# Attention block on one core: another split of the first image's preparation over the engines

## The reference

```python
h = x.reshape(B, 32, 4, N); h = (h - mu) * rsqrt(var + 1e-6)      # group norm, 32 groups of 4 channels
h = h * gamma + beta
q, k, v = w_qkv @ h + b_qkv                                        # each 128 x 1024
attn = softmax(q^T k / sqrt(128))                                  # 1024 x 1024
out = x + w_proj @ (attn @ v) + b_proj
```

## Time and profile before

| what | us |
|---|---|
| median of 3 runs | 132.26 |
| lowest, highest | 130.9, 132.26 |
| the profiled execution's own time | 131.82 |
| its span | 129.8 |
| TensorE busy in the span | 114.6 (88%) |
| VectorE, ScalarE, GpSimd busy | 93.9, 87.9, 85.4 |

### The profile page before, as it was taken

The page is one execution under the profiler, slowest core; times in us unless marked ns, Lnnn a source line. Parts: engine busy times, 40 slices in busy tenths (PEclk is TensorE's granted clock), DMA queues, the critical chain, the costliest instruction groups (busy, mean ns, idle before and its releaser), DMA issues.

```text
span 129.8 us, 3100 instructions
## 1 busy us (share of the span) xinstructions
PE 114.6 (88%) x1161; PEld 80.6 (62%) x1161; DVE 93.9 (72%) x242; ACT 87.9 (68%) x121; POOL 85.4 (66%) x60
## 2 busy tenths in 40 slices
PE   0599887988998999999989999999899999987671
PEld 0373544556775677667646776776467767767550
DVE  3659799999856967998569579776695797774222
ACT  1304429999778787877986878879868788785000
POOL 6010004879999897999759888998657666788200
PEclk9999999999999999999999999999999999999999
DMA  3692000797999999999999999999999999999990
GB/s 94 170 346 119 0 3 17 146 123 147 192 153 187 184 197 129 240 191 192 149 224 194 187 192 200 179 146 234 190 169 132 243 192 114 197 232 155 179 246 20
DMA packets 70670, 21.43 MB, mean 165 GB/s; under 512 B 68352, under 2 KB 69120, under 8 KB 70656
## 3 DMA queue, kind: packets, MB, share of 16 engines
q1 hardware_dynamic: 69888, 20.98, 89.9%
q10 hardware_dynamic: 704, 0.26, 0.8%
q0 software_dynamic: 64, 0.00, 0.0%
HBM read 2.36 MB, written 2.10 MB: 34 GB/s over the span
## 4 chain that ended last, share of the span: by engine, by line
PE 49%; DVE 23%; DMA 9%; ACT 7%; SPq 6%; issue 2%; ACTq 0%
DVE row_max L432 10%; PE scores L617 7%; DMA ptT<-p_hl 6%; PE o_ps L637 6%; PE scores L619 6%; PE scores L618 6%; PE o_ps L633 5%; PE o_ps L632 5%; SPq L232 4%; DVE t_lo L421 4%; DMA wqkv_sb<-in_L_conv_w_qkv_dram 3%; PE o_ps L643 3%; ACT probs L343 3%; DVE out_sb L453 3%; ACT p_hl L350 2%
## 5 line engine op out<-in xcount | busy, mean ns | idle before, releaser
L285 POOL TENSOR_TENSOR p_hl<-probs,p_hl 128x1024 f16<-128x1024 f32 x32 | 68.1, 2130 | 27.0 <-ACT p_hl L350 26.7
L432 DVE TENSOR_REDUCE row_max<-scores 128x1 f32<-128x1024 f32 x32 | 39.1, 1222 | 19.3 <-PE scores L619 19.1
L343 ACT ACTIVATE probs<-scores,exp_bias,esc 128x1024 f32<-128x1024 f32 x32 | 38.5, 1202 | 19.2 <-DVE exp_bias L435 19.2
L350 ACT ACTIVATE p_hl<-probs 128x1024 f16<-128x1024 f32 x32 | 33.8, 1057 | 1.0
L632 PE MATMUL o_ps<-v_hi,ptT 128*128 128x128 f16 x256 | 32.0, 219 | 0.4 <-DVE v_lo L427 0.4
L633 PE MATMUL o_ps<-v_lo,ptT 128*128 128x128 f16 x256 | 32.0, 219 | 0.0
L617 PE MATMUL scores<-z_hi,t_hi 128*128 128x512 f16 x64 | 24.3, 379 | 2.8 <-DVE t_lo L421 1.7
L632 PEld LDWEIGHTS o_ps<-v_hi,ptT 128*128 128x128 f16 x256 | 25.0, 98 | 2.3 <-issue 0.8
L633 PEld LDWEIGHTS o_ps<-v_lo,ptT 128*128 128x128 f16 x256 | 25.0, 98 | 0.2
L619 PE MATMUL scores<-z_hi,t_lo 128*128 128x512 f16 x64 | 24.3, 379 | 0.0
L618 PE MATMUL scores<-z_lo,t_hi 128*128 128x512 f16 x64 | 24.3, 379 | 0.0
(11 more groups left out here) (109 smaller groups left out, 134.0 us busy)
## 6 DMA issues: line engine op xcount, KB each, us to landing
out_dram<-out_sb SPq DMA_DIRECT2D x7, 256.0 KB, 2.6
x_sb<-in_x_dram SPq DMA_DIRECT2D x3, 512.0 KB, 4.8
ptT<-p_hl SPq DMA_TRANSPOSE x64, 3.4
x_sb<-in_x_dram SPq DMA_DIRECT2D x2, 256.0 KB, 3.3
out_dram<-out_sb SPq DMA_DIRECT2D x1, 192.0 KB, 2.0
wqkv_sb<-in_L_conv_w_qkv_dram ACTq DMA_DIRECT2D x1, 128.0 KB, 4.0
wqkv_sb<-in_L_conv_w_qkv_dram ACTq DMA_DIRECT2D x1, 64.0 KB, 3.5
wp_sb<-in_L_conv_w_proj_dram ACTq DMA_DIRECT2D x1, 64.0 KB, 3.8
```

The lines of the kernel that those rows point to most:

```text
L285: nc.gpsimd.tensor_tensor(p_hl[:, g % RING, 1], probs[:, g % RING], p_hl[:, g % RING, 0], ALU.subtract).then_inc(plo_ready, 1)
L343: nc.scalar.activation(probs[:, g % RING], scores[:, g % SLOTS], ACT.Exp, bias=exp_bias[:, g:g + 1], scale=esc[:], accum_out=row_sum[:, g: ...
L350: nc.scalar.activation(p_hl[:, g % RING, 0], probs[:, g % RING], ACT.Copy).then_inc(phi_ready, 1)
L432: nc.vector.tensor_reduce(row_max[:, g:g + 1], scores[:, g % SLOTS], AX_X, ALU.max).then_inc(max_ready, 1)
```

## The change

It rearranges the preparation of image 0 and parts of tiles 0 to 4.

- Queues: x's first half, gamma, beta, b_q, Wp and Wv are issued on SP; Wq with Wk and x's second half on ScalarE's queue.
- TensorE has six filler matmuls ahead of everything (FIRST_WARM = 6), and WARM_UP is 8. group_mean(0) moves ahead of the c products, group_var(0) ahead of Wp's transposition.
- z of image 0: ScalarE makes both high halves straight from x, with nmr = -mean * rstd as bias and rstd as scale. VectorE computes z and z_lo of the first half, GpSimd those of the second half, and nmr.
- A's high half, ct, w_mat, esc and neg_esc go from VectorE to ScalarE. g_diag, w_diag and W's halves (by way of w_n, float32) go from VectorE to GpSimd.
- t of image 0's first 128 columns is a part of its own, in `misc[:, 1, 0:P]`; the other 384 of the first half follow, and the second half comes behind score tile 0. Semaphore counts of t shift by one (t_part), those of z by z_part.
- The maximum of W, w_inv and bo move into tiles 0 and 1 of the loop.
- The v products of both halves of image 0 are together in tile 2. The statistics of image 1: channel_stats(1, 1) in tile 2 instead of 1, group_mean(1) in tile 3 instead of 2, group_var(1) in tile 4 instead of 3. One of the two KEEP_WARM groups goes.

The core of the diff (declarations, the removed counterparts on VectorE and changed counts are left out):

```diff
 def _(sp):
-    for half in range(2):
-        cols = slice(half * HALF, (half + 1) * HALF)
-        sp.dma_start(x_sb[:, cols], x_d[0, :, cols]).then_inc(x_first[half], 16)
+    w_d = w_qkv.rearrange("(t o) c -> o t c", t=3)
+    sp.dma_start(x_sb[:, 0:HALF], x_d[0, :, 0:HALF]).then_inc(x_first[0], 16)
+    sp.dma_start(gamma_c[:], col(gamma)).then_inc(gcol_loaded, 16)
...
+    sp.dma_start(wp_sb[:], w_proj).then_inc(wp_loaded, 16)
+    sp.dma_start(wqkv_sb[:, 2], w_d[:, 2]).then_inc(wv_loaded, 16)
...
-    sp.wait_ge(gcol_loaded, 16)
+    sp.wait_ge(x_first[1], 16)
...
+    pool.wait_ge(gcol_loaded, 16)
+    pool.wait_ge(consts, 1)
+    nc.gpsimd.tensor_scalar(g_diag[:], ident32[:], gamma_c[:], None, ALU.mult).then_inc(gdiag_ready, 1)
...
+    pool.wait_ge(rstd_ready, 1)
+    pool.wait_ge(mean_ready, 1)
+    nc.gpsimd.tensor_tensor(nmr[:], neg_mean[:, 0:1], rstd[:, 0:1], ALU.mult).then_inc(nmr_ready, 1)
...
+    nc.gpsimd.tensor_scalar(z32[:, HALF:N], x_sb[:, HALF:N], neg_mean[:, 0:1], rstd[:, 0:1],
+                            ALU.add, ALU.mult).then_inc(z_second, 1)
+    pool.wait_ge(z_second, 1)
+    pool.wait_ge(zhi_ready, 2)
+    nc.gpsimd.tensor_tensor(z_lo[:, HALF:N], z32[:, HALF:N], z_hi[:, HALF:N], ALU.subtract
+                            ).then_inc(zlo_second, 1)
...
+    pool.wait_ge(wmax_ready, 1)
+    nc.gpsimd.tensor_scalar(w_diag[:], ident32[:], w_max[:, 0:1], None, ALU.mult).then_inc(wdiag_ready, 1)
+    pool.wait_ge(winv_ready, 1)
+    pool.wait_ge(wmat_ready, 1)
+    nc.gpsimd.tensor_scalar(w_n[:], w_mat[:], w_inv[:], None, ALU.mult).then_inc(wn_ready, 1)
+    pool.wait_ge(wn_ready, 1)
+    nc.gpsimd.tensor_copy(w_hi[:], w_n[:]).then_inc(whi_ready, 1)
+    pool.wait_ge(whi_ready, 1)
+    nc.gpsimd.tensor_tensor(w_lo[:], w_n[:], w_hi[:], ALU.subtract).then_inc(w_ready, 1)
...
-    act.dma_start(gamma_c[:], col(gamma)).then_inc(gcol_loaded, 16)
...
-    act.dma_start(wqkv_sb[:, 2], w_d[:, 2]).then_inc(wvp_loaded, 16)
-    act.dma_start(wp_sb[:], w_proj).then_inc(wvp_loaded, 16)
+    act.dma_start(x_sb[:, HALF:N], x_d[0, :, HALF:N]).then_inc(x_first[1], 16)
...
+    act.wait_ge(nmr_ready, 1)
+    for half in range(2):
+        cols = slice(half * HALF, (half + 1) * HALF)
+        nc.scalar.activation(z_hi[:, cols], x_sb[:, cols], ACT.Identity, bias=nmr[:], scale=rstd[:, 0:1]
+                             ).then_inc(zhi_ready, 1)
+    act.wait_ge(ainv_ready, 1)
+    act.wait_ge(amat_ready, 1)
+    nc.scalar.activation(a_hi[:], a_mat[:], ACT.Copy, scale=a_inv[:]).then_inc(ahi_ready, 1)
+    act.wait_ge(craw_ready, 1)
+    nc.scalar.activation(ct[:], c_raw[:], ACT.Copy, scale=a_inv[:]).then_inc(ct_ready, 1)
...
+    nc.scalar.activation(w_mat[:], scores[:, 1, HALF:HALF + P], ACT.Copy, scale=gamma_c[:]
+                         ).then_inc(wmat_ready, 1)
...
+    act.wait_ge(t_psum, 1)
+    act.wait_ge(ct_ready, 1)
+    nc.scalar.activation(t_hi[:, 0:P], misc[:, 1, 0:P], ACT.Identity, bias=ct[:]).then_inc(thi_ready, 1)
...
+    act.wait_ge(amax_safe, 1)
+    nc.scalar.activation(esc[:], a_max[:, 2:3], ACT.Copy, scale=1.0 / math.sqrt(P)).then_inc(esc_ready, 1)
+    nc.scalar.activation(neg_esc[:], a_max[:, 2:3], ACT.Copy, scale=-1.0 / math.sqrt(P)
+                         ).then_inc(esc_ready, 1)
...
+    dve.wait_ge(z_ready, 1)
+    dve.wait_ge(zhi_ready, 1)
+    nc.vector.tensor_tensor(z_lo[:, 0:HALF], z32[:, 0:HALF], z_hi[:, 0:HALF], ALU.subtract
+                            ).then_inc(zlo_ready, 1)
...
+    dve.wait_ge(thi_ready, 1)
+    nc.vector.scalar_tensor_tensor(out=t_lo[:, 0:P], in0=misc[:, 1, 0:P], scalar=ct[:], in1=t_hi[:, 0:P],
+                                   op0=ALU.add, op1=ALU.subtract).then_inc(tlo_ready, 1)
...
         if g == 0:
+            dve.wait_ge(wmax_psum, 1)
+            nc.vector.tensor_reduce(w_max[:, 1:2], o_ps[:, 1, P:2 * P], AX_X, ALU.max).then_inc(wmax_all, 1)
+            dve.wait_ge(wmax_all, 1)
+            nc.vector.tensor_scalar(w_max[:, 2:3], w_max[:, 1:2], 1.0 / V_MAX, TINY, ALU.mult, ALU.max
+                                    ).then_inc(wmax_safe, 1)
+            dve.wait_ge(wmax_safe, 1)
+            nc.vector.reciprocal(w_inv[:], w_max[:, 2:3]).then_inc(winv_ready, 1)
+        if g == 1:
             t_low(0, 1)
-        if g == 1:
+            dve.wait_ge(bo_psum, 1)
+            dve.wait_ge(o_loaded, 32)
+            nc.vector.tensor_tensor(bo[:], bp_c[:], o_ps[:, 0, 0:1], ALU.add).then_inc(bo_ready, 1)
             channel_stats(1, 0)
+        if g == 2:
             channel_stats(1, 1)
-        if g == 2:
+        if g == 3:
             group_mean(1)
-        if g == 3:
+        if g == 4:
             group_var(1)
         if s in (2, 3) and b < B:
             v_low(b, s - 2)
                          ).then_inc(var_psum, 1)
...
+    pe.wait_ge(const_warm, 1)
+    pe.wait_ge(const_dve, 3)
+    for _ in range(FIRST_WARM):
+        nc.tensor.matmul(scores[:, 1, 0:HALF], ones16[:], warm[:], start=True, stop=True)
...
+    pe.wait_ge(const_dve, 5)
+    group_mean(0)
...
-    group_mean(0)
+    group_var(0)
...
+    pe.wait_ge(zlo_ready, 1)
+    pe.wait_ge(a_ready, 1)
+    nc.tensor.matmul(misc[:, 1, 0:P], a_hi[:], z_hi[:, 0:P], start=True, stop=False)
+    nc.tensor.matmul(misc[:, 1, 0:P], a_hi[:], z_lo[:, 0:P], start=False, stop=False)
+    nc.tensor.matmul(misc[:, 1, 0:P], a_lo[:], z_hi[:, 0:P], start=False, stop=True).then_inc(t_psum, 1)
...
+        if g == 0:
+            t_products(0, 1)
+            pe.wait_ge(wdiag_ready, 1)
+            pe.wait_ge(amax_all, 1)
+            nc.tensor.matmul(o_ps[:, 1, P:2 * P], ones32[:], w_diag[:], start=True, stop=True
+                             ).then_inc(wmax_psum, 1)
+        if g == 1:
+            pe.wait_ge(wraw_ready, 1)
+            pe.wait_ge(o_loaded, 32)
+            nc.tensor.matmul(o_ps[:, 0, 0:1], w_raw[:], beta_c[:], start=True, stop=False)
+            nc.tensor.matmul(o_ps[:, 0, 0:1], wpT[:], bv_c[:], start=False, stop=True).then_inc(bo_psum, 1)
+        if g == LAG:
+            group_var(1)
         if g > LAG:
...
-            if s in (1, 2):
-                if g < TILES:
-                    pe.wait_ge(w_ready, 2)
-                pe.wait_ge(tlo_ready, b * 2 + s)
+            if g == 2:
+                pe.wait_ge(w_ready, 1)
+                for half in range(2):
+                    pe.wait_ge(tlo_ready, t_part(0, half))
+                    v_products(0, half)
+            if s in (1, 2) and b >= 1:
+                pe.wait_ge(tlo_ready, t_part(b, s - 1))
...
-            if g in (2, 3):
-                if g == 2:
-                    group_mean(1)
-                else:
-                    group_var(1)
+            if g == 3:
+                pe.wait_ge(bo_ready, 1)
+                group_mean(1)
...
```

More of the change, by code:

```diff
@@ L30 @@
 V_MAX = 4.0
-WARM_UP = 6
+FIRST_WARM = 6
+WARM_UP = 8
 KEEP_WARM = 4
@@ L79, in attention_block @@
         c_abs = sb("c_abs", [P, 1])
+        nmr = sb("nmr", [P, 1])
+        w_n = sb("w_n", [P, P])
         ct = sb("ct", [P, 1])
@@ L143, in attention_block @@
         araw_ready = sem("araw_ready")
+        esc_ready = sem("esc_ready")
+        bo_ready = sem("bo_ready")
+        ct_ready = sem("ct_ready")
         amat_ready = sem("amat_ready")
@@ L202, in stat, with z_part, t_part @@
             return o_ps[:, 0, 2 * P + which:2 * P + which + 1] if b < 2 else misc[:, which, 0:1]
+        def z_part(b, half):
+            return b * 2 + half if b else 1
+        def t_part(b, half):
+            return b * 2 + half + 2
         def wait(eng, s, value):
@@ L326, in t_high @@
             def t_high(b, half):
[L327 to L331, removed]
+                act.wait_ge(t_psum, t_part(b, half))
+                first = P if b == 0 and half == 0 else 0
+                nc.scalar.activation(t_hi[:, b * N + half * HALF + first:b * N + (half + 1) * HALF],
+                                     misc[:, half, first:HALF], ACT.Identity, bias=ct[:]).then_inc(thi_ready, 1)
             def v_high(b, half):
@@ L418, in t_low @@
             def t_low(b, half):
[L419 to L422, removed]
+                dve.wait_ge(thi_ready, t_part(b, half))
+                first = P if b == 0 and half == 0 else 0
+                cols = slice(b * N + half * HALF + first, b * N + (half + 1) * HALF)
+                nc.vector.scalar_tensor_tensor(out=t_lo[:, cols], in0=misc[:, half, first:HALF], scalar=ct[:],
+                                               in1=t_hi[:, cols], op0=ALU.add, op1=ALU.subtract
+                                               ).then_inc(tlo_ready, 1)
             def v_low(b, half):
@@ L590, in t_products @@
             def t_products(b, half):
-                pe.wait_ge(zlo_ready, b * 2 + half + 1)
-                cols = slice(b * N + half * HALF, b * N + (half + 1) * HALF)
-                nc.tensor.matmul(misc[:, half], a_hi[:], z_hi[:, cols], start=True, stop=False)
```

(12 more changed lines are left out.)

92 lines of the change are left out of this document (26 added, 66 removed).

## The result

| | before | after |
|---|---|---|
| median of the runs, us | 131.53 (20 runs, 130.54 to 132.93) | 132.94 (20 runs, 131.79 to 133.80) |
| profiled execution, us | 131.82 | 133.07 |
| its span, us | 129.8 | 131.3 |
| first row maximum | 17.18 | 15.90 |
| last row maximum | 114.89 | 116.34 |

The ratio is 1.0105, with an interval of 1.008 to 1.013: about one percent slower. The forecast was 133.2. The last three rows of the table are the handiest reading: the start gains 1.28 us, the loop loses 2.73. From the last row maximum to the span's end it is 14.9 and 15.0, so nothing happens there.

A forecast was written before the change was run, and what follows sets the result against it. Bound by one dependent path to 17.18, VectorE and ScalarE to 27.5, then nearly gapless TensorE until 108.08. The start gains 1.4, but the late variance delays values(2) by 1.4: 131.82 + 1.4 = 133.2, range 132.4 to 134.4 (55%).

The forecast's parts named there:

- The start's gain: Image 0's preparation, up to the first row maximum: forecast at 15.8 instead of 17.18, 1.4 us earlier.
- gamma's new way: At the start, gamma queued behind x's first half, its diagonal on GpSimd: booked at 0, with 0.3 either way.
- z's new route for nothing, under the block: Image 0's z saves about a microsecond but lies under the filler block, which covers 2; booked at nothing.
- The two outcomes of the shared port: Image 0's z on VectorE and GpSimd: mutual delay between zero and one z operation, 0.54, staying under the block.
- var_eps at D0 + 12.6: Image 1's variance on VectorE starts 12.6 us behind the first row maximum (D0), at 28.4 instead of 26.37.
- the sum of 3.45: Work newly standing on VectorE between the first row maximum and image 1's var_eps, added to the 9.19 us before.
- The three queues: TensorE, GpSimd, ScalarE wait for image 1's var_eps: values(0) plus 1.0, values(2) plus 1.4 (taken), exp(4) hidden.
- One microsecond late stays so: Loop behind values(2): TensorE is full, so 1.4 us late stays 1.4 us late until SP's tail.
- The rule "end = 131.82 + D0 - 14.4": Whole kernel: end follows the first row maximum D0; the change pays only if D0 falls below 14.4.
- Rival (a): Start: early fillers raise the clock for good, first row maximum 13.0 to 13.9, time 130.9; chance 27%.
- Rival (c): TensorE idle from about 26.0 to 28.5: the clock falls there, 1.5 to 2 us more, 135; chance 10%.
- Rival (b): First V product not really held by the variance, so the start's gain arrives: 130.4; chance 8%.

The follow-up runs named there:

- e1: Changed kernel with image 1's variance (group_var(1)) on VectorE just ahead of tile 4's row maximum instead of behind it; ratio to the kernel before 0.998.
- e2: Changed kernel with image 1's statistics and both filler groups back on the tiles of the kernel before, new start kept; ratio to the kernel before 0.992.
- e4: Changed kernel with GpSimd's rstd and z of image 1 behind tile 2's low half instead of ahead of it; ratio to the kernel before 1.005.
- e3: Kernel before with image 1's variance (group_var(1)) moved behind tile 4's row maximum, in tile 4 instead of 3; ratio to the kernel before 1.024.
- e11: Changed kernel with image 1's variance ahead of tile 4's maxima and GpSimd's rstd and z behind tile 2's low half; ratio to the kernel before 0.988.
- e6: On top of e2: six fillers instead of eight ahead of t, GpSimd's second z_lo waiting for a_lo; ratio to the kernel before 0.990.
- e7: On top of e2: the six filler products at the program's start removed (FIRST_WARM = 0); ratio to the kernel before 0.995.
- e10: On top of e2: t of image 0's first half in one piece again, no part for the first tile; ratio to the kernel before 1.008.

## Why the prediction was right

- **The start's gain.** 1.4 was forecast, 1.28 measured (first row maximum 15.90, forecast 15.8), and part of this closeness is luck. The block was to start 0.53 earlier and starts 0.14 earlier (in the chain's rows, from which I took 10.18, it starts at 10.04 and not at 9.65). The term that missed is gamma's new way, which I had booked at 0 with 0.3 either way: the product with its diagonal starts at 4.99, and the profile before has it at 3.66; A's product comes at 5.57 instead of 5.16, 0.41 later, and A's maximum product at 8.82, not 8.44. gamma lands behind x's half, and GpSimd takes 0.60 for a diagonal that VectorE made in 0.28. Two things made up for it. I counted eight products of 0.427 from the chain's row, which stands 0.21 behind the block's first product; and the clock was up at 13.2, just before t's first product and 3.2 us after the chain's 10.04 instead of the 3.8 that I took, so that the part of 128 columns took 0.16 and not 0.32. Where the rise falls moves by more than that between executions (e1, e2, e4).
- **z's new route for nothing, under the block.** Right for the end, wrong in its sizes: ScalarE's z_hi takes 0.76 a half and not 0.6, GpSimd's z 0.97, a_lo 1.12, so everything was ready at 12.56 and not at 11.1. Of 2.0 us of cover 0.66 was left.
- **The two outcomes of the shared port.** The Trainium skill, "SBUF — State Buffer", section "SBUF: two separate sides", calls the pair an exclusive lock between a VectorE operation with two SBUF inputs and a GpSimd operation that reads SBUF. The trace agrees: a_lo has two, started 0.17 behind GpSimd's z_lo and ended 0.13 behind its end. This delay of 0.77 is more than the 0.54 that I gave as the bound, and the block covered it. It sat not in the price of z's low halves, where I looked for it, but in that of the small operation behind them.
- **var_eps at D0 + 12.6.** Measured D0 + 12.34: the sum of 3.45 was 0.30 too large (12.34 less 9.19 is 3.15). With D0 0.1 later it came out at 28.24 against 28.4.
- **The three queues.** First V product 28.44 (28.55 forecast), its wait ended by var_eps; p_low(2) 30.62 (30.7); SP's transpose 32.79 (32.8); values(2) 36.08 (36.05), a wait of 0.90 for the transposed half. exp(4) at 30.48, hidden as forecast. e1, e3, e4 and e11 show by edits what these rows show by times: each of the two waits costs. TensorE's wait alone was priced at 0.66, and e4, which has only that one, is 0.65 slower than before. That the low half alone would cost the whole 1.4, since values(2) waits for it until 36.08 in any case, is read from the rows; no run has that wait alone.
- **One microsecond late stays so.** Shown: from the ninth row maximum to the last it is 73.44 to 73.47 in all twelve profiles; e2, e6, e7 and e10 have a way of 98.40 with first maxima from 14.31 to 17.35.
- **The rule "end = 131.82 + D0 - 14.4"** gives 133.3 for the measured D0; the profiled execution has 133.07.
- **Rival (a), the early rise,** I held for all or nothing, at 27%. It is neither: it happens in a share of executions. In after, 2 of 20 have a mean clock of 0.987 and took 132.57 and 131.79, under the median of 132.94; no trace of those shows where the clock was low, so that they are early rises is likely and not shown. I was wrong in its extent too: in e6 and e11 the level falls again before the block, and the gain in e2 is 1.0 and not 2.
- **Rival (c), the clock's fall in the hole,** exists (e4's profile). In after three executions have means of 0.961 to 0.974, and took 133.80, 133.04 and 132.49; without their traces I can't say where it fell.
- **Rival (b)** is refuted: the loop takes back twice what the start gives, until the variance is moved.

Left open: by how much e3's median is above the expectation, gamma's 0.43 in e10, and what decides when the clock rises in one execution.

## What to carry to other kernels

A faster start is worth what the first fully loaded stretch sees of it: read there which wait ends last, and move the work that stands ahead of it on each queue before gaining on the start. A scalar of 0.14 us behind one more wide operation can cost ten times its length if three queues hang on it. Filler matmuls have two sides: they cover what is behind them, and where they end too early or leave a hole of one or two microseconds, the lower clock can come back.

## What the runs showed of the hardware

- VectorE with two SBUF inputs beside GpSimd: a_lo 1.12 us instead of 0.35, nine profiles with and one (e6) without.
- GpSimd's z of 128x512 takes 0.97 where VectorE's z runs beside it, 0.76 in the loop (1.52 for two). Its 128x128 product with a scalar takes 0.60, VectorE's 0.28.
- ScalarE's 128x512 activation with a tensor as scale and bias takes 0.76, where the plain copy takes 0.57.
- The page's granted clock reads 1.00 from the start, while 512 columns take 0.42: the first lower level isn't in it. After a rise, a fall shows as 0.50. So the spacing tells the level at the start, and a mean under 0.99 tells that the clock rose and then fell somewhere, which may belong to a faster execution or a slower one.
